# A second late token group kept turned in DRAM, and the raw second shared weights loaded behind the last expert tile

## The chip, the core and the metric

The kernel runs on one core of one Trainium2 chip. A core has TensorE (PE, matrix products, weight loads shown as PEld), VectorE (DVE), ScalarE (ACT) and GpSimd (POOL), and SyncE (SP), which here only issues transfers and counts their landings. Sixteen DMA engines carry the transfers. SBUF holds 128 partitions; matrix products land in eight PSUM banks of 128x512 values. The metric is device time in microseconds of one execution, as the median of several runs. A profiled execution gives the trace.

## What is computed

The input is 2 x 2048 tokens of 512 values (4096 tokens). Cut to what matters:

```python
# attention part (linear, no softmax over positions)
h = layernorm(X) * ln_w + ln_b;  Q, K, V = split(h @ W_in + b_in)
A = sum over positions of (K_rot / |K_rot|) * V
x = x + layernorm(X + (A * Q_rot) @ W_out + b_out)      # X = layernorm(x)
# FFN part, on xf = layernorm(x), 8 experts, the best 2 of each token
gates = softmax of the 2 largest of xf @ gate_w
routed = sum over the 2 experts of gate * (gelu(xf @ w1[e] + b1[e]) @ w2[e] + b2[e])
shared = gelu(xf @ shared_w1 + shared_b1) @ shared_w2 + shared_b2
out = x + layernorm(routed + shared)
```

`w1[e]` is 512x256, `w2[e]` 256x512, both shared weights are 512x512. Every large product is made with operands split in two parts, a high one and the rest (`_hi`, `_lo`), as three products: hi·hi, hi·lo and lo·hi.

## The kernel before

Tokens are worked on in eight groups of 512 (`G`), each of four tiles of 128. One program per engine is written out by hand, and each engine runs its own in order; semaphores (`wait_ge`, `then_inc`) tie them. Nothing reorders the work. A wait of SP holds back every transfer that SP issues behind it. The phases are:

1. **Front (to about 300 us).** Per group: normalization, transposes, K, V and Q. Expert and shared weights are split in units and stored in DRAM (`we_dram`, `ws_dram`).
2. **Middle (about 300 to 510 us), the loop `for s in range(NG)`.** Stage s makes the attention output of group s (`attend`), x2 and n3 (the FFN's input, `norm_x2`), and turns n3 of group s − 1 on PE (`n3_turn`, L1666) into `tp`; ACT copies it as `n_hi` (L761), DVE subtracts for `n_lo` (L1152). From these come the gate logits and, for the five groups in `EARLY` = (0, 2, 4, 6, 7), the shared part: h at one stage, output tiles at the next (`fill`). DVE copies each output tile into a buffer `fo` (L1186, `f_out`), and SP stores it to `f_dram` (`store_f`, L518). In the middle of the phase two `fo` buffers take turns, so the third copy of a stage waits for the first tile's store to have landed.
3. **Routing (about 510 to 565 us).** Tokens are sorted by expert into `NRT` = 72 row tiles, of which 71 are worked on.
4. **Expert phase (to about 821 us).** Per tile i: POOL gathers 128 rows, PE turns them and makes both products, ACT scales, POOL scatters with addition into `f_dram` (L1614). SP runs a loop over the tiles, waits for each scatter to land (L602), and slips in loads whose target has become free.
5. **Late phase (the last 85 us).** The shared part of the three groups in `LATE` = (1, 3, 5), called late groups 0, 1, 2, and the last normalization of all groups. `places` sets the order: h(0), h(1), o(0), h(2), o(1), o(2). h(i) has four products of 12 matmuls, written here h(i,m), each into a bank of PSUM: h(0,m) into banks 0, 1, 3, 4; for i above 0 h(i,m) into banks 3 and 4 in turn, so each waits for the gelu of the product two before it (`sc_free`). ACT makes the gelu (L887) and the high part (L891), DVE the low part (L1445). o(i) has four output tiles; each needs all of h(i) and the second shared weights in two parts (`c2_hi`, `c2_lo`). DVE adds the output tile to what lies in `f_dram` (loaded as `f[g]`, L591) and takes its statistics (L1476, L1478); ACT normalizes (L896), POOL or DVE add x2, and the result is stored.

Late group 0's turned parts, made at stage 2, are stored to `nt_dram` by SP (L527) and come back in the expert phase as `nc_hi[0]` and `nc_lo[0]`. Late groups 1 and 2 are loaded as plain n3 (`n3c`) and turned on PE in the late phase: `late_turn(1)` stands between h(0,1) and h(0,2), `late_turn(2)` between h(1,1) and h(1,2). The first shared weights come from DRAM in two parts (`c1_hi`, `c1_lo`). The second come raw, `c2_raw`, and are split by ACT (L901) and DVE (L1489) in four parts beside h(0). Space in SBUF is shared over time: the expert weights of expert e lie at 16e to 16e + 16 KB, and what the late phase loads goes there once an expert's tiles are done.

## Time and profile before

| | us |
|---|---|
| median of 3 runs | 904.56 (904.41 to 906.53) |
| profiled execution, its own time | 903.74 |
| its span | 901.9 |
| PE busy | 850.7 (94%) |
| DVE busy | 671.6 (74%) |
| ACT busy | 430.1 (48%) |
| POOL busy | 404.5 (45%) |
| HBM read and written | 118.23 MB, 93.11 MB |

The span runs from the first to the last instruction of the trace; the profiled execution's own time is 1.8 us longer than that. Busy time is the time in which an engine works on an instruction. The granted clock of PE (PEclk) is given as a share of full speed: 1.00 is 2.4 GHz, 0.50 is 1.2 GHz. In a timeline, what stands in brackets behind a row is how long the engine was idle before it and what ended that; a row without brackets followed its predecessor or waited for under 0.2 us. All times are us from the start of the span.

### The profile page before, as it was taken

The page shows a single profiled execution, that of the slowest core. Times are in us where ns is not written, and L with a number is a line of the kernel's source. Part 1 is how long each engine was busy: PE and PEld are TensorE (multiplying, and loading weights), DVE is VectorE, ACT ScalarE, POOL GpSimd, SP SyncE. Part 2 cuts the span into 40 slices and gives each one's busy share as a digit, 9 for nine tenths or more (in the row PEclk, how much of TensorE's full clock was granted, in tenths as well). Part 3 has the DMA queues.
Part 4 walks back from the last instruction along what each step waited for, and adds up shares of the span by engine and source line. Part 5 has one row for each costly group of instructions (what it writes and reads, how often), then busy time and mean ns, then how long its engine had stood idle before and what let it go on. Part 6 is the DMA issues. An engine that isn't in the chain of part 4 may idle for free.

```text
span 901.9 us, 14793 instructions
## 1 busy us (share of the span) xinstructions
PE 850.7 (94%) x4510; PEld 712.6 (79%) x4510; DVE 671.6 (74%) x1446; ACT 430.1 (48%) x815; POOL 404.5 (45%) x322
## 2 busy tenths in 40 slices
PE   4999999999999989999999885999999999999986
PEld 3888888878888778788888664888888888888865
DVE  6977989889879887687778596566666656665877
ACT  5235445336242243242413471566666666666564
POOL 1457567576565010000001001567677667762275
PEclk9999999999999999999999988999999999999998
DMA  9228878778749798758533988588888879888999
GB/s 322 98 104 314 296 263 328 268 284 315 252 158 401 309 382 308 288 209 324 187 129 102 398 324 264 107 220 166 142 142 170 197 155 166 148 136 203 370 250 220
DMA packets 88026, 212.30 MB, mean 235 GB/s; under 512 B 11576, under 2 KB 20024, under 8 KB 82576
## 3 DMA queue, kind: packets, MB, share of 16 engines
q1 hardware_dynamic: 63520, 166.61, 50.6%
q0 software_dynamic: 19360, 43.60, 26.3%
q10 hardware_dynamic: 5072, 1.15, 0.8%
q8 instruction: 41, 0.67, 0.3%
q14 instruction: 33, 0.27, 0.1%
HBM read 118.23 MB, written 93.11 MB: 234 GB/s over the span
## 4 chain that ended last, share of the span: by engine, by line
PE 55%; DVE 19%; issue 8%; DMA 6%; ACT 6%; POOL 5%; DVEq 0%; POOLq 0%; SPq 0%; ACTq 0%
PE bank L1671 6%; PE bank L1672 6%; PE bank L1673 6%; PE bank L1916 4%; PE bank L1901 4%; PE bank L1915 3%; PE bank L1914 3%; PE bank L1933 3%; PE bank L1931 3%; PE bank L1932 3%; DMA n_scratch<-picked 2%; DVE rot L976 2%; PE bank L1666 2%; PE bank L1923 2%; POOL rsn L1548 2%
## 5 line engine op out<-in xcount | busy, mean ns | idle before, releaser
L1614 POOL DMA_INDIRECT f_scratch<-ro,dst x71 | 112.5, 1585 | 54.5 <-SPq L602 24.7
L1606 POOL DMA_INDIRECT xr<-n_scratch,ids x71 | 70.2, 989 | 71.9 <-issue 44.1
L1408 DVE TENSOR_TENSOR ro<-bank,b2b 128x512 f32<-128x512 f32 x71 | 49.1, 692 | 67.6 <-PE bank L1933 55.7
L1671 PE MATMUL bank<-wkv_hi,h_hi 128*128 128x512 f32 x248 | 97.2, 392 | 0.0
L1673 PE MATMUL bank<-wkv_hi,h_lo 128*128 128x512 f32 x248 | 96.6, 389 | 0.0
L1672 PE MATMUL bank<-wkv_lo,h_hi 128*128 128x512 f32 x248 | 96.5, 389 | 0.0
L1914 PE MATMUL bank<-we,x_hi 128*128 x284 | 86.1, 303 | 0.5 <-DVE x_lo L1383 0.5
L667 ACT ACTIVATE sq<-kb 128x512 f32<-128x512 f32 x32 | 20.3, 634 | 130.1 <-DVE kb L979 130.1
L1916 PE MATMUL bank<-we,x_lo 128*128 x284 | 80.4, 283 | 0.0
L1915 PE MATMUL bank<-we,x_hi 128*128 x284 | 80.4, 283 | 0.0
L1541 POOL TENSOR_TENSOR acc<-acc,prod 128x512 f32<-128x512 f32 x32 | 57.6, 1798 | 8.7 <-DVE prod L992 8.7
L1383 DVE TENSOR_TENSOR x_lo<-bank,x_hi 128x512 fp32r<-128x512 f32 x71 | 49.1, 691 | 11.4 <-ACT x_hi L837 9.4
L1587 POOL TENSOR_TENSOR zr<-zv,half 128x4 f32<-128x4 f32 x8 | 8.1, 1010 | 109.0 <-DVE zv L1122 109.0
L1931 PE MATMUL bank<-we,g_hi 128*128 x142 | 56.3, 396 | 0.7 <-DVE g_lo L1395 0.7
L1534 POOL TENSOR_TENSOR rn<-ssq,half 128x1 f32<-128x1 f32 x32 | 27.7, 866 | 64.1 <-ACT sq L667 64.1
L1933 PE MATMUL bank<-we,g_lo 128*128 x142 | 56.4, 397 | 0.0
L1932 PE MATMUL bank<-we,g_hi 128*128 x142 | 56.0, 394 | 0.0
L1914 PEld LDWEIGHTS bank<-we,x_hi 128*128 128x128 f32 x284 | 54.0, 190 | 0.9 <-issue 0.9
L1673 PEld LDWEIGHTS bank<-wkv_hi,h_lo 128*128 128x128 f32 x248 | 46.5, 188 | 9.7
L1915 PEld LDWEIGHTS bank<-we,x_hi 128*128 128x128 f32 x284 | 54.2, 191 | 0.0
L1671 PEld LDWEIGHTS bank<-wkv_hi,h_hi 128*128 128x128 f32 x248 | 46.6, 188 | 9.6
L1672 PEld LDWEIGHTS bank<-wkv_lo,h_hi 128*128 128x128 f32 x248 | 46.6, 188 | 9.3
(248 smaller groups left out, 2490.7 us busy)
## 6 DMA issues: line engine op xcount, KB each, us to landing
xg<-in_X SPq DMA_DIRECT2D x15, 1024.0 KB, 7.9
we<-expert_scratch SPq DMA_DIRECT2D x6, 2048.0 KB, 13.6
w_lo<-in_w SPq DMA_DIRECT2D x16, 512.0 KB, 5.5
expert_scratch<-w_hi SPq DMA_DIRECT2D x16, 512.0 KB, 2.8
expert_scratch<-w_lo SPq DMA_DIRECT2D x16, 512.0 KB, 4.2
q_scratch<-qh SPq DMA_DIRECT2D x8, 1024.0 KB, 3.9
q_scratch<-qb SPq DMA_DIRECT2D x8, 1024.0 KB, 6.1
q_hi<-q_scratch SPq DMA_DIRECT2D x8, 1024.0 KB, 4.8
```

The source lines that it names most:

```text
L1541: pool.tensor_tensor(a, a, prod[j % 2][:, :], ALU.add).then_inc(acc_done, 1)
L1606: pool.indirect_dma_start(xr[u][:, :], None, n3_dram, bass.IndirectOffsetOnAxis(ids[:, i:i + 1], 0)).then_inc(row_in[u], 16)
L1614: pool.indirect_dma_start(f_dram, bass.IndirectOffsetOnAxis(dst[:, i:i + 1], 0), ro[i % NRO][:, :], None, compute_op=ALU.add).then_inc(r_s ...
L1671: pe.matmul(dst, hi(k), w_hi(k), start=(k == 0), stop=False)
L1672: pe.matmul(dst, hi(k), w_lo(k), start=False, stop=False)
L1673: last = pe.matmul(dst, lo(k), w_hi(k), start=False, stop=(k == KD - 1 and not more))
L1914: pe.matmul(out_h, x_hi[u][:, s], part_of(e, 0, k, H), start=(k == 0), stop=False)
L1915: pe.matmul(out_h, x_hi[u][:, s], part_of(e, 1, k, H), start=False, stop=False)
L1916: last = pe.matmul(out_h, x_lo[u][:, s], part_of(e, 0, k, H), start=False, stop=(k == KD - 1))
L1931: pe.matmul(oe_ps[u][:, :], g_hi[u][:, s], part_of(e, 2, k, D), start=(k == 0), stop=False)
L1932: pe.matmul(oe_ps[u][:, :], g_hi[u][:, s], part_of(e, 3, k, D), start=False, stop=False)
L1933: last = pe.matmul(oe_ps[u][:, :], g_lo[u][:, s], part_of(e, 2, k, D), start=False, stop=(k == KH - 1))
```

## The change

It does four things.

- **Stores.** Late group 1 (token group 3) is treated at stage 4 as late group 0 is at stage 2: its `n_hi` and `n_lo` are stored to `nt_dram`, which has a place for two groups. ACT waits for these stores before it writes `n_hi` of group 4.
- **Loads.** In place of the plain n3 of late group 1, four pieces of 512 KB of the turned parts are loaded at tiles 64 to 67 of SP's loop. `late_turn(1)`, its ACT copies and its DVE subtractions are gone. `nc_hi[1]` and `nc_lo[1]` move to 16 and 24 KB, `f[2]` and `f[3]` to 164 and 96 KB.
- **Raw second weights.** `c2_raw` moves from 16 to 80 KB. It is loaded behind SP's loop over the tiles and behind a wait for the last tile's product, where it was loaded at tile 66. It is split beside h(0,2), h(0,3), h(1,0) and h(1,1), where it was beside h(0,0) to h(0,3). The high part of late group 2 (`nc_hi[2]`, also at 80 KB) waits for the split.
- **Waits of SP.** The loads of `f` follow without waits for the split and for the transposes.

```diff
@@ placement
-        f = [at(f"f{g}", kb_, [P, GT, D]) for g, kb_ in enumerate((64, 104, 16, 24, 32, 40, 48, 56))]
-        n3c = [None, at("n3c1", 8 * LATE[1], [P, GT, D]), at("n3c2", 72, [P, GT, D])]
-        nc_hi, nc_lo = (... for n, kbs in (("nc_hi", (128, 164, 80)), ("nc_lo", (0, 96, 88))))
+        f = [at(f"f{g}", kb_, [P, GT, D]) for g, kb_ in enumerate((64, 104, 164, 96, 32, 40, 48, 56))]
+        n3c2 = at("n3c2", 72, [P, GT, D])
+        nc_hi, nc_lo = (... for n, kbs in (("nc_hi", (128, 16, 80)), ("nc_lo", (0, 24, 88))))
-        c2_raw = at("c2_raw", 8 * EARLY[1], [P, KS, D])
+        c2_raw = at("c2_raw", 80, [P, KS, D])
+        c2_in = {("h", 0, 2): (0,), ("h", 0, 3): (1,), ("h", 1, 0): (2,), ("h", 1, 1): (3,)}
@@ SP, stages of the middle
-                if s == LATE[0] + 1:
-                    sp.wait_ge(t2_free, 2 + t2_use(LATE[0], KD - 1) + 1)
+                if s - 1 in LATE[:2]:
+                    sp.wait_ge(t2_free, 2 + t2_use(s - 1, KD - 1) + 1)
                     for c, part in enumerate((n_hi, n_lo)):
-                        sp.dma_start(nt_dram[c], ...).then_inc(turned, 16)
+                        sp.dma_start(nt_dram[LATE.index(s - 1), c], ...).then_inc(turned, 16)
@@ SP, loop over the tiles and behind it
                 if i == NRT - E:
                     sp.wait_ge(oe_full, NRT - E)
-                    load_n3(1)
-                if i == NRT - E + 2:
-                    sp.dma_start(c2_raw[:, :, :], sw2.rearrange("(k p) d -> p k d", p=P)).then_inc(c_in[1], 16)
+                if i in range(NRT - E, NRT - E + 4):
+                    c, h = (i - NRT + E) // 2, (i - NRT + E) % 2 * 2
+                    sp.dma_start((nc_hi, nc_lo)[c][1][:, h:h + 2, :]..., nt_dram[1, c, :, h * G:(h + 2) * G]).then_inc(n3c_in[1], 16)
+            sp.wait_ge(oe_full, NRT - 1)
+            sp.dma_start(c2_raw[:, :, :], sw2.rearrange("(k p) d -> p k d", p=P)).then_inc(c_in[1], 16)
...
             load_f(EARLY[0])
             load_f(LATE[0])
-            sp.wait_ge(c_split, KS)
             for g in EARLY[1:]:
                 load_f(g)
-            sp.wait_ge(tc_full, KD)
             load_f(LATE[1])
             load_f(LATE[2])
-            sp.wait_ge(tc_full, KD * (len(LATE) - 1))
+            sp.wait_ge(tc_full, KD)
@@ ACT
-                    if g == LATE[0] + 1 and k == 0:
-                        act.wait_ge(turned, 32)
+                    if g - 1 in LATE[:2] and k == 0:
+                        act.wait_ge(turned, 32 * (LATE.index(g - 1) + 1))
...
             scale_row(PRE)
-            for k in range(KD):
-                nc_hi_part(1, k)
-            act.dma_start(n3c[2][:, :, :], n3_groups[LATE[2]]).then_inc(n3c_in[2], 16)
+            act.dma_start(n3c2[:, :, :], n3_groups[LATE[2]]).then_inc(n3c_in[2], 16)
             for what, i, m in places:
                 if what == "h":
                     gelu_c(i, m)
-                if (what, i) == ("h", 0):
-                    c2_hi_part(m)
+                for k in c2_in.get((what, i, m), ()):
+                    c2_hi_part(k)
@@ DVE
-            nc_lo_parts(1)
...
                 if what == "h":
                     hc_lo_part(i, m)
-                    if i == 0:
-                        c2_lo_part(m)
+                    for k in c2_in.get((what, i, m), ()):
+                        c2_lo_part(k)
@@ PE, late_h
                     pe.wait_ge(oe_free, 2 + NRT - 1)
-                    late_turn(1)
...
-                pe.wait_ge(tc_free, 4 + KD * i)
+                if i == 1:
+                    pe.wait_ge(n3c_in[1], 64)
+                else:
+                    pe.wait_ge(tc_free, KD)
```

How this stands in the programs is shown at three places. Line numbers of the changed kernel are about three higher for the same line.

SP at stage 4 of the middle phase, before. `fo0` is the buffer of output tile (2,0):

```order
L452 DMA q_hi0_162<-q_scratch 128x2048 [waits o_full]
L452 DMA q_lo0_160<-q_scratch 128x2048
L532 DMA we_233<-expert_scratch 128x2x1024 [waits zero_stored]
L518 DMA f_scratch<-fo0_178 128x512 [waits o_free]
L518 DMA f_scratch<-fo1_179 128x512 [waits o_free]
L538 DMA out_0<-z0_157 128x4x512 [waits x2_ready]
```

and in the changed kernel:

```order
L455 DMA q_hi0_162<-q_scratch 128x2048 [waits o_full]
L455 DMA q_lo0_160<-q_scratch 128x2048
L530 DMA turned_scratch<-n_hi_167 128x2048 [waits t2_free]
L530 DMA turned_scratch<-n_lo_168 128x2048
L535 DMA we_233<-expert_scratch 128x2x1024 [waits zero_stored]
L521 DMA f_scratch<-fo0_178 128x512 [waits o_free]
L521 DMA f_scratch<-fo1_179 128x512 [waits o_free]
L541 DMA out_0<-z0_157 128x4x512 [waits x2_ready]
```

The two stores of 1 MB stand ahead of the half expert load and of the output tiles' stores.

SP at the end of its loop over the tiles, before (`r_stored` counts landed scatters by buffer):

```order
L588 DMA n3c1_264<-n3_scratch 128x4x512 [waits r_stored3,r_stored0,r_stored1,r_stored2,oe_full]
L618 DMA c2_raw_284<-in_shared_w2 128x4x512 [waits r_stored1,r_stored2]
L591 DMA f0_256<-f_scratch 128x4x512 [waits r_stored3,r_stored0,r_stored1,r_stored2]
L591 DMA f1_257<-f_scratch 128x4x512
L591 DMA f2_258<-f_scratch 128x4x512 [waits c_split]
```

and in the changed kernel:

```order
L619 DMA nc_hi1_266<-turned_scratch 128x1024 [waits r_stored3,r_stored0,r_stored1,r_stored2,oe_full]
L619 DMA nc_hi1_266<-turned_scratch 128x1024 [waits r_stored1]
L619 DMA nc_lo1_269<-turned_scratch 128x1024 [waits r_stored2]
L619 DMA nc_lo1_269<-turned_scratch 128x1024 [waits r_stored3]
L622 DMA c2_raw_283<-in_shared_w2 128x4x512 [waits r_stored0,r_stored1,r_stored2,oe_full]
L591 DMA f0_256<-f_scratch 128x4x512
L591 DMA f1_257<-f_scratch 128x4x512
```

The loop's last waits for scatters, which stood at f0, stand at `c2_raw` now.

ACT at the start of the late phase, from the last scaled row, before. `hsc` is a gelu's result, `bank4` here is that of h(0,3):

```order
L856 ACTIVATE ro2_254<-ro2_254,gate_of_96 128x512 [waits gate_ready,oe_free,oe_full]
L864 ACTIVATE nc_hi1_267<-bank7 128x512 [waits tc_full]
L864 ACTIVATE nc_hi1_267<-bank2 128x512 [waits tc_full]
L864 ACTIVATE nc_hi1_267<-bank5 128x512 [waits tc_full]
L864 ACTIVATE nc_hi1_267<-bank6 128x512 [waits tc_full]
L907 DMA n3c2_265<-n3_scratch 128x4x512
L887 ACTIVATE hsc0_276<-bank0,sb1c_56 128x512 [waits sc_full]
L891 ACTIVATE hc_hi0_278<-hsc0_276 128x512 [waits sc_free]
L901 ACTIVATE c2_hi_274<-c2_raw_284 128x512 [waits c_in1]
L887 ACTIVATE hsc1_277<-bank1,sb1c_56 128x512 [waits sc_full]
```

and in the changed kernel, where the first rows are `L859` and the load of `n3c2`:

```order
L892 ACTIVATE hsc0_275<-bank0,sb1c_56 128x512 [waits sc_full]
L896 ACTIVATE hc_hi0_277<-hsc0_275 128x512 [waits sc_free]
L892 ACTIVATE hsc1_276<-bank1,sb1c_56 128x512 [waits sc_full]
L896 ACTIVATE hc_hi0_277<-hsc1_276 128x512 [waits sc_free]
L892 ACTIVATE hsc0_275<-bank3,sb1c_56 128x512 [waits hc_split,sc_full]
L896 ACTIVATE hc_hi0_277<-hsc0_275 128x512 [waits sc_free]
L906 ACTIVATE c2_hi_273<-c2_raw_283 128x512 [waits c_in1]
L892 ACTIVATE hsc1_276<-bank4,sb1c_56 128x512 [waits hc_split,sc_full]
L896 ACTIVATE hc_hi0_277<-hsc1_276 128x512 [waits sc_free]
```

The first copy of the second weights stands behind h(0,2) and ahead of the gelu of h(0,3).

## Rows read from the trace of the kernel before

**Rows 1.** Busy time by stretch: stretch, length, PE, PEld, DVE, ACT, POOL, PEclk, DMA, GB/s

```profile
430.00:500.00 70.00, 69.11 (x334) 56.93 (x332) 52.92 (x158) 23.95 (x37) 6.42 (x6) 1.00 0.44 156
```

**Rows 2.** Timeline of SP at stage 2: start, length, queue, line, transfer

```profile
349.45 0.33 SPq L452 DMA_DIRECT2D q_hi<-q_scratch  x1
...
350.30 0.43 SPq L527 DMA_DIRECT2D turned_scratch<-n_hi  x1
...
354.79 3.99 SPq L518 DMA_DIRECT2D f_scratch<-fo  x2
```

**Rows 3.** Timelines of DVE and PE at the end of stage 2

```profile
363.80 0.69 DVE L1186 COPY fo<-bank 128x512 f32<-128x512 f32 x1 [2.85 <-DMA f_scratch<-fo]
...
370.26 1.09 PE L1666 MATMUL bank<-ident,n 128*128 128x128 f32 x8 [1.48 <-ACT n L773]
```

**Rows 4.** Timeline of SP at stage 4

```profile
404.57 0.33 SPq L452 DMA_DIRECT2D q_hi<-q_scratch  x1
...
405.43 0.43 SPq L532 DMA_DIRECT2D we<-expert_scratch  x1
409.98 3.99 SPq L518 DMA_DIRECT2D f_scratch<-fo  x2
```

**Rows 5.** Timelines of DVE, ACT and PE at the end of stage 4

```profile
416.06 0.67 DVE L1186 COPY fo<-bank 128x512 f32<-128x512 f32 x1
...
419.52 2.94 ACT L773 ACTIVATE n<-z,xnm,xr__76 128x512 f32<-128x512 f32 x4 [12.52 <-DVE xnm L1145]
...
423.75 1.03 PE L1666 MATMUL bank<-ident,n 128*128 128x128 f32 x8
```

**Rows 6.** Busy time by stretch, at stage 4 (columns as in rows 1)

```profile
410.00:415.00 5.00, 5.00 (x22) 4.04 (x22) 4.02 (x8) 0.00 (x0) 0.00 (x0) 1.00 1.01 384
```

**Rows 7.** Timeline of SP at the end of the expert phase

```profile
812.07 0.37 SPq L588 DMA_DIRECT2D n3c<-n_scratch  x1
816.88 0.38 SPq L618 DMA_DIRECT2D c_raw<-in_shared_w  x1
833.23 12.87 SPq L591 DMA_DIRECT2D f<-f_scratch  x8
```

**Rows 8.** Chain of work that ended last, in order of time: start, length, what

```profile
825.04 8.10 DMA f_scratch<-ro,dst
...
833.23 5.60 DMA f<-f_scratch
```

**Rows 9.** Timeline of ACT beside h(0)

```profile
827.98 0.62 ACT L901 ACTIVATE c_hi<-c_raw 128x512 fp32r<-128x512 f32 x1
828.50 0.67 ACT L887 ACTIVATE hsc<-bank,sb1c 128x512 f32<-128x512 f32 x1
```

**Rows 10.** Timeline of PE: late_turn(1), h(0,2), h(1,1), o(0) and its second tile

```profile
824.13 1.91 PE L1666 MATMUL bank<-ident,n3c 128*128 128x128 f32 x16
825.79 0.48 PE L1974 MATMUL bank<-nc_hi,c_hi 128*128 128x512 f32 x1
...
834.05 0.39 PE L1974 MATMUL bank<-nc_hi,c_hi 128*128 128x512 f32 x1
...
843.98 0.39 PE L1671 MATMUL bank<-c_hi,hc_hi 128*128 128x512 f32 x1
...
846.70 0.39 PE L1671 MATMUL bank<-c_hi,hc_hi 128*128 128x512 f32 x1
```

**Rows 11.** Timeline of DVE: low part of h(1,3), first add of a late tile

```profile
846.05 0.67 DVE L1445 TENSOR_TENSOR hc_lo<-hsc,hc_hi 128x512 fp32r<-128x512 f32 x1
...
848.35 0.68 DVE L1476 TENSOR_TENSOR f<-bank,f 128x512 f32<-128x512 f32 x1
```

**Rows 12.** Busy time by stretch, around two falls of PE's clock (columns as in rows 1)

```profile
554.00:560.00 6.00, 0.00 (x0) 0.00 (x0) 1.04 (x5) 0.00 (x0) 2.41 (x3) 0.56 0.92 353
560.00:565.00 5.00, 4.23 (x18) 3.52 (x19) 2.53 (x4) 1.20 (x2) 0.00 (x0) 0.51 0.52 207
875.00:879.00 4.00, 3.73 (x9) 2.97 (x10) 3.35 (x12) 0.26 (x1) 3.58 (x5) 0.57 1.12 222
```

More of the change, by code:

```diff
@@ L244, in sandwich_kernel @@
         rank_ps, ids_ps = bank[2], bank[0]
-        tc = ((bank[7], bank[2], bank[5], bank[6]), (bank[1], bank[0], bank[7], bank[2]))
+        tc = (bank[1], bank[0], bank[7], bank[2])
         sc = (bank[0], bank[1], bank[3], bank[4])
@@ L523, in _ @@
                     load_q(s + 2)
-                if s == LATE[0] + 1:
-                    sp.wait_ge(t2_free, 2 + t2_use(LATE[0], KD - 1) + 1)
+                if s - 1 in LATE[:2]:
+                    sp.wait_ge(t2_free, 2 + t2_use(s - 1, KD - 1) + 1)
                     for c, part in enumerate((n_hi, n_lo)):
-                        sp.dma_start(nt_dram[c], part[:, :, :].rearrange("p k t -> p (k t)").bitcast(F32)).then_inc(turned, 16)
+                        sp.dma_start(nt_dram[LATE.index(s - 1), c], part[:, :, :].rearrange("p k t -> p (k t)").bitcast(F32)).then_inc(turned, 16)
                 if s in (3, 4):
@@ L595, in _ @@
             sp.wait_ge(f_stored[0], 16 * f_buf_uses[0])
[L596 to L597 removed]
+            sp.wait_ge(turned, 64)
+            sp.dma_start(nc_hi[0][:, :, :].rearrange("p k t -> p (k t)").bitcast(F32), nt_dram[0, 0]).then_inc(turned, 16)
             sp.dma_start(c1_hi[:, :, :].rearrange("p k h -> p (k h)").bitcast(F32), ws_dram[0, 0]).then_inc(turned, 16)
@@ L860, in scale_row_before, with nc_hi_part @@
                     scale_row(i - 2)
-            def nc_hi_part(i, k):
-                act.wait_ge(tc_full, KD * (i - 1) + k + 1)
-                act.activation(nc_hi[i][:, k, :], tc[i - 1][k][:, :], ACT.Copy).then_inc(nc_hi_done, 1)
+            def nc_hi_part(k):
+                act.wait_ge(tc_full, k + 1)
+                if k == 0:
+                    act.wait_ge(c_split, KS)
+                act.activation(nc_hi[2][:, k, :], tc[k][:, :], ACT.Copy).then_inc(nc_hi_done, 1)
             x_hi_part(0, 0)
@@ L1937, in expert @@
                 return pe.value_load(owner[0:1, i:i + 1], min_val=0, max_val=E - 1)
-            def late_turn_part(i, k):
-                pe.wait_ge(tc_free, KD * (i - 1) + k + 1)
-                transposes(tc[i - 1][k], n3c[i], k).then_inc(tc_full, 1)
             x_turn(0, 0, 0)
@@ L1958, in _, with late_turn @@
             h_turn(PRE, PRE % 2)
-            def late_turn(i):
-                pe.wait_ge(n3c_in[i], 16)
+            def late_turn():
+                pe.wait_ge(n3c_in[2], 16)
                 for k in range(KD):
-                    late_turn_part(i, k)
+                    transposes(tc[k], n3c2, k).then_inc(tc_full, 1)
             def late_h_part(i, m, lo):
@@ L1978, in _ @@
             pe.wait_ge(xt_free, PRE + 1)
-            pe.wait_ge(turned, 64)
+            pe.wait_ge(turned, 96)
             pe.wait_ge(c_in[0], 64)
```

31 lines of the change are left out of this document (14 added, 17 removed).

## The prediction, made before the changed kernel ran

> **What bounds the kernel now.** I read the busy shares by stretch first, then the timelines of SyncE (SP, which issues most transfers) and of the engines behind it, and last the chain of work that ended last. In the middle phase TensorE (PE) is the bound: it is busy 69.11 of the 70 us from 430 to 500 [rows 1], so an idle gap put into it there is not made up before the routing, and the routing and the 71 expert tiles follow it. The last 85 us are different. Their chain goes through the landing of the last scatter at 833.2 and the landing of f0 at 838.8 [rows 8], and then mostly through VectorE (DVE). PE works without a gap across that landing, since its late products need neither. So a shorter PE list at the end is worth little by itself; a new wait for something that lands near 838 is worth much.
>
> **Part 1, two more stores at stage 4.** SP now sends group 3's n_hi and n_lo (1 MB each) between the loads of q for stage 6 and the half expert load `we`. Issuing one costs SP 0.43 us [rows 2], about 1 for both, and no engine waits for that. What counts is what stands behind them: the 256 KB store of output tile (2,0). DVE's third copy of that stage writes the same buffer and waits for that store to land. Stage 2 already does the same thing, so its rows give the price. There q was issued at 349.45, the stores of the turned rows at 350.30 and after, the tile's store at 354.79 [rows 2], and DVE's copy waited 2.85 us and ran at 363.80 [rows 3]. That is 9.0 us after the issue of a 256 KB transfer, and 14.35 us after the q loads: the small store landed behind 4 MB.
>
> Stage 4 has the same line-up with `we` (1 MB) as well. From the q loads at 404.57 [rows 4]: 14.35, plus 1.05 MB at 384 GB/s [rows 6], 2.7 us, gives a landing at 421.6. From the other side: the copy at 416.06 ran without a wait [rows 5], so the store had landed by then; 2.10 MB more at 384 GB/s adds 5.5, at most 421.5. I take 421.5, so the copy is 5.4 us late. Behind it in DVE's list stand the last statistics, then GpSimd's root, ScalarE's (ACT) four normalizations and PE's transposes of them. At stage 2 the transposes began 370.26 − 363.80 = 6.46 us after the late copy, and PE had stood idle for 1.48 [rows 3]. At stage 4: 421.5 + 6.46 = 427.96, against 423.75 now with no gap [rows 5]. **PE stands idle 4.2 us**; between landings of 420.5 and 422.5 that is 3.2 to 5.2.
>
> A stall costs clock too. After a short gap the granted clock fell, near 875, from full (2.4 GHz) to half (1.2): the mean of 0.57 over four us is 3.4 us at half [rows 12], which loses 1.7. After the 6 us without a matmul from 554, the five that followed had 0.51, 4.9 us at half, a loss of 2.45 [rows 12]. For 4.2 us I take 1.7; I keep 0 to 2.45, as I can't tell from these rows what falls into a gap of this length. **Part 1: +5.9 us** (3.2 to 7.6). The wait that the change adds on ACT (group 4's n_hi must not be written before group 3's has left) comes after those same transposes, at 427.96 or later, when the stores, which stand ahead of the tile's store, have landed: 0, and what hides it is PE's gap.
>
> The trace and a price of the Trainium skill part here. DMA: Bandwidth & Descriptors, section "Anatomy of one DMA", gives a transfer of the GpSimd path about 2.0 us plus its bytes at 436 GB/s; read as the price of any transfer by itself, that is an estimate of 2.6 us for 256 KB, part 1 would be 0 and the sum 7.0 us. The section "Queues, rings and completion order" of that page of the Trainium skill says that each DMA engine takes a ring's entries in order and that the mark of completion lands after all earlier writes of that engine, and the 9.0 us of stage 2 agree with that.
>
> **Part 2, the second late group loaded ready-made.** Gone: 16 transposes on PE (824.13 to 825.79, 1.66 us [rows 10]), four ACT copies of 0.62 [rows 9] and four DVE subtractions, on engines that wait for PE there. In their place SP loads four pieces of 512 KB at tiles 64 to 67 instead of one 1 MB group and the 1 MB of raw weights. The first goes at 812.07 and the third at 816.88 [rows 7], the last between that and the end of the loop. It needs to be there when product h(1,0) begins. From h(1,1) at 834.05 to the first output tile at 843.98 stand three products and 1.66 of transposes [rows 10], so a product is 2.76 us; h(1,0) began at 831.3 and would now at 829.7. If it is late it is covered, since PE is held up anyway until 840 (below): 0. ACT issues the load of the third group's n3 directly behind the last scaled row, sooner than before, and the transposes that need it come later than before: 0.
>
> **Part 3, the raw second weights.** This decides. Before, `c2_raw` was issued at 816.88, in the loop [rows 7]. Now it stands behind the loop, and the loop's last pass waits for tile 70's scatter to land. That is where SP stands until 833.23, when it issues f0 [rows 7, 8]; the wait for the last tile's product that the diff writes there has then long been met. So the raw weights are issued at 833.23. A 1 MB load from there lands after 5.60 us, by f0's own: **838.8** [rows 8]. I keep 837.5 to 841, since the traffic ahead changes and eight f loads follow behind. By the same page and section of the Trainium skill, DMA: Bandwidth & Descriptors (2.0 us and 1.05 MB at 436 GB/s), it would be an estimate of 4.4 us, and the sum 1.2 less; I keep the row.
>
> ACT reaches the first `c2_hi` copy behind the gelu and the copy of h(0,2). PE has that product one product ahead of 829.7, at 827.0; gelu 0.67 and copy 0.62 [rows 9] make it 828.3, where ACT now stands until 838.8 (before, this copy ran at 827.98 with its data there). Queued behind it: the gelu of h(0,3). PE can do h(0,3) and h(1,0), but h(1,1) writes the bank that this gelu reads. So PE stops at 834.05 − 1.66 = 832.4 and goes on at 838.8 + 0.52 (copy) + 0.67 (gelu) + 0.1 = **840.1**; it began h(1,1) at 834.05 [rows 9, 10]. That is 6.05 late, with the 1.66 saved already in it. The stall of 7.7 us should drop the clock; between the two cases above, 2.1 us is lost after it, so PE begins the first output tile near 843.98 + 8.15 = 852.1. DVE hangs on that by ACT's gelu and copy of h(1,3), 1.3 together: 853.4, against 846.05 for that subtraction [rows 11], +7.4. DVE's first add of a late tile ran at 848.35, some 1.3 us after its product was done (PE had begun the next at 846.70) [rows 10, 11]. That lag shrinks, and takes up a little of the delay: +7.0 at that add, from where the tail is DVE's as before. The four subtractions of c2 (0.7 each, as the add of such a tile [rows 11]) fall into the time in which DVE waits for PE's late products, so they add nothing. f0 lands another 1.05 MB at 384 GB/s later, 2.7 us, at 841.5, and its first statistics stand behind three of the c2 copies and two gelus, near 843.5: no wait. **Part 3: +7.0 us**; without the clock's share and with a landing at 837.5 it is 3.6, with one at 841 and 2.45 of clock 9.5.
>
> **The sum:** 5.9 + 7.0 = 12.9 us. The profiled execution's own time is 903.74 (span 901.9), so 916.6 on that; the median of the runs is 904.56, so **917.4** for the median.
>
> **Rivals.**
> Only the end stalls (B): transfers of one queue overtake each other, so that the tile's store lands as it does alone. For it: the store at 409.98 had landed within 6.1 us behind 3 MB of loads [rows 4, 5]. Against: stage 2, where the stall of 2.85 is there [rows 3]. Time: 904.56 + 7.0 = 911.6.
> Only the middle stalls (C): the last scatter lands early enough, since less traffic runs beside it, and `c2_raw` is on the chip by about 831. It would have to end 7 us sooner than the 8.10 us it takes [rows 8]. Time: 904.56 + 5.9 = 910.5, perhaps less a little.
> Not slower (D): SP issues `c2_raw` once the last product is done, as the diff's own wait reads; that is before PE's transposes at 824.13 [rows 10], so it lands by 829.7; with the tile's store unhindered too, PE keeps its 1.66 us. It decides from a landing at 831.1 (832.4 less 1.3); every us later is one us of PE stall. Time: 904.56 − 1.66 = 902.9. Against: program order on SP, and the fact that f0, which follows the same last wait, was issued at 833.23 [rows 7].
> More than the forecast (E): the clock stays at half longer after both stalls, or the scatter shares its engines with the 512 KB pieces and lands later: 921 and above.
>
> **How the numbers follow.** Both stalls (A) 0.78, B 0.10, C 0.05, D 0.04, E 0.03. A runs from 6.8 us (3.2 + 3.6) to 17.1 (7.6 + 9.5), 911.4 to 921.7; its upper end needs every term at its worst. With B and C at 911.6 and 910.5 taken in, the range is 909.5 to 921.0, which leaves out D, E and a corner of A, under 2 in 10. A measurement of this kernel tells about 0.3% (2.7 us) from no change: A, B, C and E are slower, 0.94 with a little of each lost to the bound; D at 902.9 is within it, 0.04; 0.02 is left for faster.
>
> **What the profile of the changed kernel would show.** DVE's third `fo` copy of stage 4 waits 4 to 6 us for f_scratch<-fo; PE has a gap of about 4 us ahead of the next transposes, near 424, and half clock after it. The expert phase is as long as before, shifted by some 6 us. `c_raw` is issued in one row with f0, about 8 us behind the last scatter's issue. ACT's first c_hi waits some 10 us for a DMA, and PE has a gap of about 7.7 us ahead of an L1971 matmul with a release by ACT's gelu. I am wrong if the copy of stage 4 runs without a wait, if `c_raw` goes out well ahead of f0, or if the tail behind the first late add is shorter by more than 2 us than the 53.5 us from 848.35 to the end now.

## The result, and the profile after

The changed kernel takes 919.37 us (median of five runs, 914.83 to 920.9), the kernel before beside it 904.56 us (five runs, 904.09 to 906.53). The ratio is 1.0151, with an interval of 1.0128 to 1.0175: 13.7 us slower by the ratio. The forecast was 917.4, in a range of 909.5 to 921.0. The profiled execution of the changed kernel took 914.83, the lowest of the five, with a span of 912.9 (before: 901.9). Its rows show both stalls, and beside them an expert phase that was 3.3 us shorter than before.

Stage 4, SP, in the order of issue (start, us, engine and line, operation, out<-in, count). It answers to [rows 4]:

```profile
404.42 0.33 SPq L455 DMA_DIRECT2D q_hi<-q_scratch  x1
404.79 0.43 SPq L455 DMA_DIRECT2D q_lo<-q_scratch  x1
405.27 0.43 SPq L530 DMA_DIRECT2D turned_scratch<-n_hi  x1
405.74 0.65 SPq L530 DMA_DIRECT2D turned_scratch<-n_lo  x1
406.44 0.45 SPq L535 DMA_DIRECT2D we<-expert_scratch  x1
409.83 3.99 SPq L521 DMA_DIRECT2D f_scratch<-fo  x2
```

DVE and PE behind it, which answer to [rows 5]:

```profile
422.88 0.69 DVE L1189 COPY fo<-bank 128x512 f32<-128x512 f32 x1 [6.89 <-DMA f_scratch<-fo]
...
423.62 0.50 PE L1672 MATMUL bank<-wo_hi,q_hi 128*128 128x512 f32 x1 [2.59 <-DVE fo L1189]
...
429.33 1.09 PE L1667 MATMUL bank<-ident,n 128*128 128x128 f32 x8 [1.09 <-ACT n L776]
```

The store goes out at 409.83 and the copy that needs its buffer runs at 422.88, after a wait of 6.89 us; before it ran at 416.06 without one. PE has two gaps, 3.68 us in all. The first one I had not named: the next group's attention product wants the bank that the late copy empties. The transposes begin at 429.33, before at 423.75: 5.6 us.

The end of the expert phase and the late phase. SP, ACT and PE, answering to [rows 7], [rows 9] and [rows 10]:

```profile
815.30 1.60 SPq L619 DMA_DIRECT2D nc_hi<-turned_scratch  x2
819.79 4.69 SPq L619 DMA_DIRECT2D nc_lo<-turned_scratch  x2
836.07 0.38 SPq L622 DMA_DIRECT2D c_raw<-in_shared_w  x1
836.50 14.94 SPq L591 DMA_DIRECT2D f<-f_scratch  x8
...
841.18 0.63 ACT L906 ACTIVATE c_hi<-c_raw 128x512 fp32r<-128x512 f32 x1 [10.26 <-DMA c_raw<-in_shared_w]
...
842.44 0.79 PE L1971 MATMUL bank<-nc_hi,c_hi 128*128 128x512 f32 x1 [7.47 <-ACT hsc L892]
```

The raw weights are issued in one breath with f0. ACT stands 10.26 us for them, PE 7.47 us behind ACT's gelu. In the chain that ended last, the load of the raw weights (the second row below) now follows the last scatter (the first row), where f0 stood in [rows 8]; the others are the stretch behind the stall:

```profile
828.59 7.39 DMA f_scratch<-ro,dst
836.07 5.10 DMA c_raw<-in_shared_w
...
849.35 0.69 DVE hc_lo L1447
850.04 0.61 DVE c_lo L1491
850.74 0.61 ACT nc_hi L869
851.37 2.48 DVE nc_lo L1415 x4
```

Clock and traffic by stretch (from:to, length, busy us and count for PE, PEld, DVE, ACT and POOL, PEclk, DMA share, GB/s), answering to [rows 1] and [rows 12]:

```profile
424.00:428.00 4.00, 4.00 (x12) 2.86 (x10) 3.83 (x25) 1.66 (x3) 1.01 (x1) 0.58 0.82 319
430.00:500.00 70.00, 69.88 (x340) 58.01 (x339) 55.24 (x142) 22.13 (x35) 5.73 (x6) 1.00 0.41 148
842.00:848.00 6.00, 5.56 (x14) 4.29 (x15) 3.73 (x6) 3.30 (x7) 0.00 (x0) 0.51 1.02 388
875.00:879.00 4.00, 3.17 (x14) 2.27 (x14) 3.40 (x12) 2.87 (x5) 2.81 (x3) 1.00 1.10 181
```

The clock is at half behind both stalls: 0.58 over 424 to 428 is 3.4 us at half, which loses 1.7; after the late stall it is at half for some 5.2 us. From 430 to 500 PE is as dense as before.

### The profile page after: what moved, and what is told of

The parts are those of the page before. It is cut to its first block, busy times and chain, and to the rows that moved or that the text cites. A ratio compares the mean times of both kernels' runs of the same rounds, so it can differ in the third digit from the quotient of the medians.

```text
span 912.9 us, 14757 instructions
## 1 busy us (share of the span) xinstructions
PE 851.4 (93%) x4494; PEld 713.2 (78%) x4494; DVE 667.3 (73%) x1442; ACT 428.1 (47%) x811; POOL 404.7 (44%) x322
## 4 chain that ended last, share of the span: by engine, by line
PE 53%; DVE 19%; DMA 9%; issue 7%; ACT 6%; POOL 5%; POOLq 0%; DVEq 0%; ACTq 0%; SPq 0%
PE bank L1672 6%; PE bank L1673 6%; PE bank L1674 6%; PE bank L1932 3%; PE bank L1916 3%; PE bank L1917 3%; PE bank L1915 3%; PE bank L1934 3%; PE bank L1902 3%; PE bank L1933 3%; DMA f_scratch<-fo 2%; DMA n_scratch<-picked 2%; DVE rot L979 2%; DMA f_scratch<-ro,dst 2%; PE bank L1667 2%
## 5 line engine op out<-in xcount | busy, mean ns | idle before, releaser
L1411 DVE TENSOR_TENSOR ro<-bank,b2b 128x512 f32<-128x512 f32 x71 | 49.1, 692 | 73.5 <-PE bank L1934 68.5
L1672 PE MATMUL bank<-wo_hi,q_hi 128*128 128x512 f32 x128 | 52.2, 408 | 5.1 <-DVE fo L1189 2.6
L776 ACT ACTIVATE n<-z,xnm,xr__76 128x512 f32<-128x512 f32 x32 | 23.4, 804 | 67.2 <-DVE xnm L1148 67.2
## 6 DMA issues: line engine op xcount, KB each, us to landing
we<-expert_scratch SPq DMA_DIRECT2D x6, 2048.0 KB, 13.5
```

Source lines behind the costliest of these rows:

```text
L1672: pe.matmul(dst, hi(k), w_hi(k), start=(k == 0), stop=False)
```

## The experiments

Eleven kernels were timed beside the kernel before, and that kernel was profiled once more (c2). The kernel before had medians of 907.4, 906.2 and 907.1 in the three groups of runs, above the 904.56 of the first comparison, so each number is read against its own group: e1, e2, e3 and e6 against 907.4; c1, e5, e7 and e8 against 906.2; e9, e10, e11 and c2 against 907.1. A difference in us below is the ratio less one, times 906.

One table serves for all. It splits each profiled execution at two instants: the first transposes of the expert phase on PE, and L, SP's first issue behind its loop, which comes once the last scatter has landed. The last two columns are timed.

| kernel | expert phase begins | from there to L | L to the end | median | against before (interval) |
|---|---|---|---|---|---|
| before | 560.31 | 272.9 | 68.7 | 904.56 | |
| before once more (c2) | 563.23 | 271.5 | 71.4 | 907.1 | |
| changed | 566.42 | 269.7 | 76.8 | 919.37 | 1.0151 (1.0128 to 1.0175) |
| changed once more (c1) | 568.62 | 269.6 | 77.2 | 919.59 | 1.0149 (1.0122 to 1.0177) |
| e1 raw at tile 68 | 568.68 | 272.5 | 77.3 | 921.77 | 1.0160 (1.0123 to 1.0197) |
| e2 turned stores behind | 556.72 | 276.5 | 77.5 | 912.29 | 1.0048 (1.0029 to 1.0068) |
| e3 part 1 alone | 569.03 | 273.7 | 70.7 | 913.36 | 1.0066 (1.0045 to 1.0088) |
| e5 before, stores behind | 558.12 | 269.5 | 70.5 | 902.07 | 0.9955 (0.9937 to 0.9974) |
| e6 raw by ACT | 568.21 | 277.6 | 69.9 | 915.65 | 1.0079 (1.0050 to 1.0108) |
| e7 raw at tile 66 | 568.33 | 272.1 | 68.5 | 912.34 | 1.0065 (1.0044 to 1.0086) |
| e8 = e7 and stores behind | 558.48 | 271.7 | 68.5 | 901.10 | 0.9944 (0.9927 to 0.9962) |
| e9 part 2 alone | 560.12 | 277.8 | 68.6 | 909.24 | 1.0034 (1.0015 to 1.0052) |
| e10 turned stores by POOL | 566.47 | 277.2 | 75.8 | 920.43 | 1.0144 (1.0117 to 1.0171) |
| e11 raw behind f0 | 570.60 | 273.1 | 79.2 | 924.84 | 1.0201 (1.0174 to 1.0228) |

The kernels whose small store waits at stage 4 begin the expert phase at 566.4 to 570.6, the others at 556.7 to 563.2. From L to the end it is 75.8 us or more where the raw weights land late, and 71.4 or less in the others. The middle column varies by 8 us from one trace to the next; what the edits do to it is taken up with e9.

### The change again, and the kernel before again

> The changed kernel once more, unaltered, as the yardstick for the runs beside it. The kernel before ran at 907.4 beside the first four experiments, 2.8 us above the 904.6 of the first comparison. Theory (the 1.5% is a property of the change): 12 to 16 us above the kernel before, whatever that measures here. In its trace the stage 2 gap of PE decides a part: 1.68 us left the clock at full (transposes of the next stage 26.7 us later), 2.1 us and more in the three experiments dropped it (28.3 us).

> The kernel before, unaltered, for a second trace of it. Beside the experiments it measured 906 to 907, against 904.6 in the first comparison. Theory: PE's gap ahead of 370 is above 2 us here and drops the clock, so the next transposes begin 28.3 us later instead of 26.7, and the expert phase starts near 562.5 instead of 560.3. Rival: the difference lies in the expert phase alone.

c1 is 13.5 us above the kernel before (11.1 to 16.0): the result repeats. c2 is a single execution, 908.02 us; the 907.1 in its row of the table is the median of its group. The first of these rows is c2's, the second c1's:

```profile
371.17 1.51 PE L1666 MATMUL bank<-ident,n 128*128 128x128 f32 x8 [2.28 <-ACT n L773]
```

```profile
370.86 1.09 PE L1667 MATMUL bank<-ident,n 128*128 128x128 f32 x8 [2.26 <-ACT n L776]
```

And the stretch 368 to 376 of both, c2 first:

```profile
368.00:376.00 8.00, 5.72 (x23) 4.48 (x23) 7.17 (x14) 4.12 (x6) 0.00 (x0) 0.79 0.67 251
```

```profile
368.00:376.00 8.00, 5.74 (x34) 4.58 (x33) 7.90 (x13) 4.70 (x8) 0.00 (x0) 1.00 0.66 250
```

In c2 the gap of stage 2 is 2.28 us, the clock drops to half (0.79 as the mean of the stretch), and the next transposes come at 399.47, 28.3 us later. That is what the theory said. Against the first trace these transposes are 2.5 us later, and the start of the expert phase is 2.9 us later. So in this pair of traces stage 2 explains most of the difference at that point; that it explains the medians too, 2 to 3 us higher here, isn't shown by one more trace. In c1 a gap of 2.26 us left the clock at full (next transposes 26.7 us later). Over all traces with a gap of 2.1 to 2.5 there, the clock fell in c2, e1, e3, e6 and e11 and stayed in c1 and e7; with 1.48 to 1.76 (before, changed, e9) it stayed. So my expectation that everything over 2.1 us drops it was too simple.

### Part 1 alone (e3)

```diff
-                if s == LATE[0] + 1:
-                    sp.wait_ge(t2_free, 2 + t2_use(LATE[0], KD - 1) + 1)
+                if s - 1 in LATE[:2]:
+                    sp.wait_ge(t2_free, 2 + t2_use(s - 1, KD - 1) + 1)
                     for c, part in enumerate((n_hi, n_lo)):
-                        sp.dma_start(nt_dram[c], ...)
+                        sp.dma_start(nt_dram[LATE.index(s - 1), c], ...)
```

(on the kernel before; ACT's wait goes with it)

> The kernel before with part 1 alone: group 3's turned rows are stored at stage 4 as in the changed kernel and ACT waits for them, but nothing reads them; late group 1 is still turned on PE and the raw weights are loaded at tile 66. Theory: the middle is 5.6 us longer, as in the changed kernel; 904.6 becomes 910.2. Rival (the expert phase takes back about 3 us of a later start, as its rows in the changed kernel read): 907 to 908. Rival (parts overlap, the middle costs nothing at the end): 904.6.

Measured: 6.0 us slower (4.1 to 8.0). In its trace the third copy waits:

```profile
425.25 0.69 DVE L1186 COPY fo<-bank 128x512 f32<-128x512 f32 x1 [6.79 <-DMA f_scratch<-fo]
```

The late phase is untouched: 70.7 us from L, where the kernel before has 68.7 and 71.4. The loss arrives whole at the end, and the rival by which the expert phase takes half of it back falls. It had come from the changed kernel's first profile: its 269.7 us from the start of the expert phase to L (269.6 in c1) are at the low end of what the table shows, and e5, which has no stall, has 269.5.

### The stores behind the first two output tiles (e2, e5)

```diff
-                if s - 1 in LATE[:2]:
-                    ...                      # the stores of the turned rows
...
                 for g in late:
                     store_f(g, 0)
                     store_f(g, 1)
+                if s - 1 in LATE[:2]:
+                    ...                      # the same lines
```

> The changed kernel with the stores of the turned rows issued behind the stores of the stage's first two output tiles instead of ahead of them, at stages 2 and 4; all else as changed. Theory (the 256 KB store lands behind what was issued ahead of it on its queue): the third fo copy of stage 4 runs without a wait near 417, PE's two gaps before 430 and the half clock behind them go, about 5.6 us at stage 4, and the wait of 2.85 us at stage 2 goes too, with PE's 1.5 us there; 919.4 becomes about 912, or less. Rival (the delay comes from total traffic, whatever the order): the copy still waits about 4 us or more and the time stays near 919. Second rival: the middle gains 5 to 7 us but the expert phase gives half of it back, 915 to 916.

> The kernel before with one edit: at stage 2 the stores of group 1's turned rows are issued behind the stores of the first two output tiles. No part of the change is in it. Theory (a small store waits for what is ahead of it on its queue): the third fo copy near 361 does not wait, PE's gap ahead of 370 goes, and the expert phase starts 3.5 us earlier: 3 to 4 us below the kernel before. Rival (the expert phase, whose length varied by 6 us between executions, swallows it): no measurable difference.

e2 is 4.3 us above the kernel before where c1 is 13.5: 9.2 us of the changed kernel's time were the place of these stores on SP, at both stages. Not all of that is the change's cost, since the kernel before has the stores of stage 2 in the same place (e5 below). SP and DVE at stage 4 of e2:

```profile
408.19 3.99 SPq L521 DMA_DIRECT2D f_scratch<-fo  x2
412.23 0.43 SPq L539 DMA_DIRECT2D turned_scratch<-n_hi  x1
412.70 0.45 SPq L539 DMA_DIRECT2D turned_scratch<-n_lo  x1
...
414.27 0.67 DVE L1189 COPY fo<-bank 128x512 f32<-128x512 f32 x1
```

The copy runs without a wait, 6.1 us after the store's issue. e2's expert phase begins at 556.7, before even the kernel before (560.3), because stage 2's own stall is gone too. e5 shows that alone: the kernel before with stage 2's stores moved is 4.1 us faster (2.4 to 5.7). That leaves some 5 of the 9.2 us for stage 4, in line with e3's 6.0.

```profile
360.81 0.67 DVE L1186 COPY fo<-bank 128x512 f32<-128x512 f32 x1
...
368.57 1.04 PE L1666 MATMUL bank<-ident,n 128*128 128x128 f32 x8
```

Against [rows 3]: the copy at 360.81 instead of 363.80, the transposes at 368.57 without a gap instead of 370.26. The stage-2 row on which I priced part 1 was at the same time a place to save.

### Is it the queue? (e10)

```diff
-                (the stores of the turned rows on SP)
...
             for s in range(NG):
                 z_rsqrt(s)
+                if s - 1 in LATE[:2]:
+                    pool.wait_ge(t2_free, 2 + t2_use(s - 1, KD - 1) + 1)
+                    for c, part in enumerate((n_hi, n_lo)):
+                        pool.dma_start(nt_dram[LATE.index(s - 1), c], ...).then_inc(stored, 16)
                 x2_rsqrt(s)
```

> The changed kernel with the stores of the turned rows issued by POOL, on its own queue, behind its root of the stage's z (near 352 and 408), ahead in time of the output tile's store on SP's queue as before, but not ahead of it in that queue. Theory (what holds the small store back is the order within one queue): the third fo copy of stage 4 does not wait, or under 1 us; 919.6 becomes about 911. Rival (the sixteen engines serve whatever was issued first, whatever queue it is on, as much traffic stands ahead): the copy waits 4 us or more, and the time stays near 919.

The theory falls. POOL's issues, SP's issue of the small store, and DVE's copy:

```profile
406.38 0.60 POOL L1596 DMA_DIRECT2D turned_scratch<-n_hi  x1
406.97 0.53 POOL L1596 DMA_DIRECT2D turned_scratch<-n_lo  x1
...
408.63 3.99 SPq L521 DMA_DIRECT2D f_scratch<-fo  x2
...
421.41 0.69 DVE L1185 COPY fo<-bank 128x512 f32<-128x512 f32 x1 [6.62 <-DMA f_scratch<-fo]
```

The copy comes 12.8 us after the store's issue, in the changed kernel 13.05, and the time is the changed kernel's (1.0144 against 1.0149). The 2 MB on another queue hold the small store back as much as those on its own. The transfers issued from 400 on show why, with their median times to landing:

```profile
q_lo<-q_scratch SPq DMA_DIRECT2D x1, 1024.0 KB, 8.1
we<-expert_scratch SPq DMA_DIRECT2D x1, 1024.0 KB, 15.9
turned_scratch<-n_hi POOLq DMA_DIRECT2D x1, 1024.0 KB, 10.8
turned_scratch<-n_lo POOLq DMA_DIRECT2D x1, 1024.0 KB, 14.0
```

`we`, issued at 404.07 ahead of POOL's two, lands near 420, after 15.9 us, and POOL's land at 417 and 421. In the trace of the kernel before `we` landed 9.4 us after its issue. So transfers that left later on another queue held it back by 6.5 us: the queues share the DMA engines, and `we` and the small store behind it advance at a part of the rate. What counts is how many bytes are on their way beside the small store, on whichever queue. The Trainium skill says the same, DMA: Bandwidth & Descriptors, section "Issuing engines are not separate DMA queues": transfers of the scalar, sync and gpsimd engines end up on the same 16 DMA engines and interleave there. e10's row agrees, with 12.8 us.

At stage 2 the move did change something. POOL's two stores left at 352.45 and 353.22 there, some 2.5 us later than SP's, the copy waited 1.69 us (3.63 in c1), and PE's gap ahead of the transposes almost closed:

```profile
368.95 1.09 PE L1667 MATMUL bank<-ident,n 128*128 128x128 f32 x8 [0.31 <-ACT n L772]
```

That is why e10 begins the expert phase 2.1 us ahead of c1. The median, with an uncertainty of over 2 us, doesn't show it.

### The raw second weights (e1, e7, e6, e11)

e1 and e7 load them inside SP's loop, to another place in SBUF, and split them beside h(0,0) to h(0,3) as before; SP waits for the split again behind its third load of `f`. The two differ in the tile.

```diff
+                if i == NRT - E + 2:         # e7; e1 has NRT - E + 4
+                    sp.wait_ge(oe_full, NRT - E + 2)
+                    sp.dma_start(c2_raw[:, :, :], ...).then_inc(c_in[1], 16)
...
-            sp.wait_ge(oe_full, NRT - 1)
-            sp.dma_start(c2_raw[:, :, :], ...).then_inc(c_in[1], 16)
```

> Undoes part 3 alone: the raw second shared weights are loaded in SP's loop at tile 68, to the place of f[4], and split beside h(0,0) to h(0,3) as before the change; stores and loads of the turned rows stay as changed. Theory (the late stall is one mechanism, worth 7 us at the first late add): c_hi runs without a wait, no gap ahead of the L1971 matmul, and the median falls from 919.4 to about 912. Rival (the stall is covered, because the tail is DVE's and the last scatter's anyway): 917 or more. A third reading, that the ready-made group saves its 1.66 us at the end as well, would give about 910.5.

> Part 3 undone, in the way e1 should have been: the raw second shared weights are loaded at tile 66 of SP's loop, as in the kernel before, to the place of f[4], and split beside h(0,0) to h(0,3). In e1 SP reached tile 68 only at 836.9, since the last three scatters are issued and land together. Theory (the late stall is the raw weights' landing): c_hi without a wait, first late add 15 to 17 us after the last scatter's landing instead of 23.5, 8 us less than the changed kernel. Rival (part 2's pieces of 512 KB, not the raw weights, make the end late): 3 us less or nothing.

e1 won nothing (14.5 us above the kernel before), and its trace says why: tile 68 isn't early.

```profile
836.88 0.38 SPq L623 DMA_DIRECT2D c_raw<-in_shared_w  x1
841.13 15.66 SPq L591 DMA_DIRECT2D f<-f_scratch  x8
...
843.93 0.63 ACT L908 ACTIVATE c_hi<-c_raw 128x512 fp32r<-128x512 f32 x1 [11.64 <-DMA c_raw<-in_shared_w]
```

The scatters of tiles 68 to 70 can only go once an earlier tile's rows have landed (POOL waits 4.9 to 7.3 us there in every trace). They then go out within 4.2 us of one another, and in e1 SP gets past tile 68's landing and tile 70's 4.3 us apart, some 8 us after the issue of each. A load tied to tile 68 leaves 4.3 us ahead of f0; in the kernel before, at tile 66, it left 16 us ahead [rows 7]. At tile 66 (e7) it leaves at 824.26, 16 us ahead of f0, and c_hi runs at 833.36, before the scatter has landed. ACT still waits 4.9 us there, against the expectation, yet L to the end is 68.5, the lowest of the table: in the chain DVE's first statistics follow f0's landing, as before the change (the second row below). e7 is 5.9 us above the kernel before (4.0 to 7.8), c1 13.5: part 3 costs 7.6 us.

```profile
833.36 0.63 ACT L908 ACTIVATE c_hi<-c_raw 128x512 fp32r<-128x512 f32 x1 [4.89 <-DMA c_raw<-in_shared_w]
...
845.88 0.69 DVE L1470 BATCH_NORM_STATS2 fst<-f 128x6 f32<-128x512 f32 x1 [2.44 <-DMA f<-f_scratch]
```

e6 leaves the place and the split as changed and lets ACT issue the load behind the last scaled row:

```diff
+            act.dma_start(c2_raw[:, :, :], ...).then_inc(c_in[1], 16)
             act.dma_start(n3c2[:, :, :], n3_groups[LATE[2]]).then_inc(n3c_in[2], 16)
```

> The changed kernel with one transfer moved: ACT issues the load of the raw second weights, on its own queue, right behind the last scaled row and ahead of the load of the third late group's n3, instead of SP behind its loop. The split stays beside h(0,2) to h(1,1). Theory (SP's place behind the landing of the last scatter is the cause): issued near 824.5 it lands near 830, c_hi waits less than 1 us, PE's gap of 7.5 us goes; 919.4 becomes about 912. Rival (the transfer is slowed by the last scatters, whatever queue it is on): it lands near 835 and half of the gain is left, 915 to 916.

```profile
832.30 0.38 ACTq L907 DMA_DIRECT2D c_raw<-in_shared_w  x1
...
841.89 0.63 ACT L903 ACTIVATE c_hi<-c_raw 128x512 fp32r<-128x512 f32 x1 [2.85 <-DMA c_raw<-in_shared_w]
```

PE's gap is gone and L to the end is 69.9, so the late stall goes as the theory says; the load takes 9.6 us beside the last scatters, as the rival says of the transfer. By the ratios the time is 6.3 us below c1's, where e7 is 7.6 below; c_hi still waits 2.85 us, not under 1. The difference of 1.3 us is within the uncertainty of over 2 us that such a difference has, so theory and rival aren't told apart by the time, and one trace whose expert phase is among the longest doesn't do it either.

e11 exchanges two issues, f0 and the raw weights:

> The changed kernel with the raw second weights and f0 in the other order: SP issues f0 first behind the last scatter's landing, then the raw weights. Theory (what the late phase waits for is the raw weights): they land 2.7 to 5 us later than in the changed kernel, c_hi waits that much longer, and the time rises by 2.7 to 5 us to 922 to 925, although f0 is there sooner. Rival (the late phase waits for f0, the raw weights are beside it): the time falls by 2 to 3 us.

```profile
843.72 0.37 SPq L591 DMA_DIRECT2D f<-f_scratch  x1
844.14 0.50 SPq L626 DMA_DIRECT2D c_raw<-in_shared_w  x1
...
852.01 0.63 ACT L905 ACTIVATE c_hi<-c_raw 128x512 fp32r<-128x512 f32 x1 [13.01 <-DMA c_raw<-in_shared_w]
...
853.26 0.80 PE L1970 MATMUL bank<-nc_hi,c_hi 128*128 128x512 f32 x1 [10.22 <-ACT hsc L891]
```

c_hi waits 13.01 us and PE 10.22. In the first trace of the changed kernel it was 10.26 and 7.47, in c1's 11.34 and 8.55: 1.7 to 2.75 more in both. L to the end is 2.0 to 2.4 us longer, and the median 4.7 us above c1. f0's earlier landing gives nothing back. With the raw weights behind the last scatter, it is they that the late phase waits for, not f0.

### Part 2 alone, and both repairs together (e9, e8)

e9 is e7 without the stores of stage 4. Its pieces read late group 0's rows in `nt_dram`, so it leaves out late group 1's own rows and doesn't compute the result; it serves for its time alone.

> Part 2 alone: the kernel before with late group 1 loaded ready-made in four pieces at tiles 64 to 67 and its transposes, copies and subtractions gone, the raw weights at tile 66. Nothing more is stored at stage 4; the pieces read group 0's turned rows, so late group 1's shared part is computed from group 0's rows and is not the reference's. Theory (part 2 is worth 0, because the late phase hangs on the last scatter's landing and not on PE): within 1 us of the kernel before. Rival (the 1.66 us of PE transposes are saved at the end): 1.7 us below. Rival (the pieces delay the last scatters): 1 to 3 us above.

> e7 and e2 together: the raw weights at tile 66, and the stores of the turned rows behind the stores of the first two output tiles at stages 2 and 4. If the two stalls are separate their gains add: the changed kernel less 8 and less 9.5, which is 3 to 5 us below the kernel before, since stage 2's own wait goes too. Rival (they overlap, or the late phase hangs on the last scatter's landing, which the pieces delay by 1 to 3 us): level with the kernel before.

e9 is 3.1 us above the kernel before (1.4 to 4.7), so the theory of 0 misses and the rival by which the pieces delay the last scatters, 1 to 3 us above, fits. But the same part measured in other company costs nothing: e7 less e3 is −0.1, e8 less e5 −1.0, both with an uncertainty of over 2 us. At the median part 2 is worth between −1 and 3 us. That the 1.66 us of transposes are not saved is clear from e9 alone; the other two pairs leave room for it.

The traces show two things that take the saving back. In e7, e8 and e9 PE stands 2.13, 1.53 and 1.90 us ahead of h(1,0) for the last of the four pieces, which SP issues behind the raw weights; e9's row is

```profile
833.96 0.50 PE L1973 MATMUL bank<-nc_hi,c_hi 128*128 128x512 f32 x1 [1.90 <-DMA nc_lo<-turned_scratch]
```

And the last scatters are later. With 3 MB loaded at tiles 64 to 67 instead of 2, POOL's wait ahead of tile 68 and the time from the last scatter's issue to L are together 16.3, 15.9 and 16.4 us (e7, e8, e9). In the four traces with 2 MB and no pieces (before, c2, e3, e5) they are 13.2, 10.5, 11.8 and 11.9, in the other seven 13.1 to 15.4. Against that the way from L to the first late add is 15.0 us in all three, and with the transposes 15.1, 17.9, 17.2 and 17.0. In c2 and e5 the chain runs through PE's products and through both sets of transposes up to that add; this is c2's second set:

```profile
841.86 1.75 PE bank L1666 x16
```

So with part 2 the last landing came later in these traces, and what follows it sooner. How much is left at the end isn't settled by these runs: the phase ahead of it varies by more, 277.8 us up to L in e9 and 272.1 and 271.7 in e7 and e8 with the same pieces.

e8 is 5.1 us below the kernel before (3.4 to 6.6) and 18.5 us below the changed kernel beside it (c1), the fastest of the study. It is level with e5, the kernel before with four lines moved: the intervals overlap almost wholly. So the two stalls are separate and their repairs add up, and with both repaired the change still gains nothing that can be told from e5.

## Why the prediction was right, and where its steps were off

**The sum.** 12.9 us were forecast, 13.5 to 13.7 measured. Part 1 alone measures 6.0 (forecast 5.9), part 3 as c1 less e7 7.6 (forecast 7.0), part 2 between −1 and 3 (forecast 0); each has an uncertainty of about 2 us or more. Both stalls came where they were forecast and for the reason given. That the sum is right to within 1 us is in part luck, as the next paragraphs show.

**Part 1, the landing.** Forecast: the copy at 421.5, 5.4 us late. Measured 422.88, with a stage that ran 0.15 us earlier: 6.8 us late. Two terms were off and nearly cancelled. The landing was priced at 384 GB/s from the bytes issued up to the small store; it took another 1.4 us. From 404 to the copy 6.4 MB moved (339 GB/s over 18.88 us), and up to the small store 5.5 MB had been issued, so transfers issued behind it moved too. And 6.46 us were carried from stage 2 for the way from the copy to the transposes; here it is 429.33 − 422.88 = 6.45, but of the 4.2 us of idle PE only 3.7 are idle, since PE stood still earlier, for its bank, and then ran a product at half clock in the time I had counted as idle. The forecast of 4.2 idle and 1.7 of clock, 5.9, stands against 5.6 at 429.33, with the clock's 1.7 inside. The reason I gave for it, that the small store landed behind its own queue, was incomplete: e10 shows that bytes on another queue count the same. The sum had been made from bytes, so it survived this.

**Part 2, 0.** It held for the changed kernel, where PE is held up from h(1,1) on anyway. The more general premise, that the chain there goes mostly through DVE and PE's list is worth little, was read from one trace and isn't true of each: in c2, the same kernel, the chain goes through PE and both sets of transposes. And 0 was the right size without that stall too, for reasons I had not named: PE's wait of 1.5 to 2.1 us for the last piece, and later scatters (e9 above).

**Part 3, the issue.** SP issues the raw weights with f0, as forecast; landing after 5.10 us (5.60 forecast), c_hi's wait 10.26 (10.5), PE's gap 7.47 (7.7). h(1,1) begins 6.37 us after L, before 0.82 us after: 5.6 late, forecast 6.05. Then the mis-sized terms: the clock at half lasts from 842.4 to 847.6 and loses 2.6 instead of 2.1, and DVE's lag takes nothing back. I had put the four subtractions of c2 (the low parts, `c_lo`) at nothing. They are not: the chain has `c_lo` at 850.04 ahead of `nc_hi` (ACT must not write over the raw weights) and `nc_lo` behind it, and from 851.37 DVE works without a gap up to the first late add. From h(1,1) to that add are 17.2 us instead of 14.3. At the add the delay against L is 8.5, forecast 7.0. The 8.5 is one pair of traces; c1's add comes 22.7 us after L, against 15.1 to 17.9 in the four traces of kernels without parts 2 and 3.

**The tail as before.** From the first late add to the end 53.2 us (54.5 in c1), before 53.5. It held. The fall of the clock near 875 [rows 12] is absent after the change: the gap ahead of it, 1.83 us up to 875.27, is there again, 1.83 us up to 886.57, but the clock stays at full.

**The expert phase, as long as before.** In the profiled execution it was not: 3.3 us shorter up to L, which fits that this execution took 914.83 where the median is 919.37. Over fourteen traces this stretch takes 269.5 to 277.8 us whatever the edit. What makes it vary is open, but for the later last scatters of e7, e8 and e9. A single profile would have led me to believe that the expert phase returns half of the first stall; e3's median says it returns nothing.

**The rivals.** B (transfers of one queue overtake one another) and C (the scatter lands early) fall by the rows above. D (the raw weights go out by the last product) falls by the issue at 836.07. The estimate of 2.6 us for the small store was made from the price in the Trainium skill, DMA: Bandwidth & Descriptors, section "Anatomy of one DMA", read as that of any transfer by itself. It falls with B: the copy ran 13.05 us after the issue.

## What to carry to other kernels

A small store whose buffer is soon needed again should be issued ahead of every megabyte that can wait. Here that order alone decided 9 us of the changed kernel's time, of which 4 us were already lost in the kernel that was taken as tuned; changing the queue instead of the order gained nothing that the time shows. A load that sits behind a loop over landings is as late as the last landing, however early its own condition was met, and small moves in the list weigh much: the exchange with its neighbour f0 cost 4.7 us (e11), and two tiles sooner in the loop were worth 8.6 (e7 against e1): read where the issuing engine stands, not what the wait says. And where one stretch of a kernel varies by more than the effect, split each trace at fixed events, and leave the judgement of that stretch to medians.

## What the runs showed of the hardware

- A 256 KB store that leaves 4.6 us after the last of 3 MB of loads was done within 6.1 us; with 2 MB more issued ahead of it, 13.05 us passed until the copy that needed it (12.8 when those 2 MB were on POOL's queue). A 1 MB load issued ahead of POOL's 2 MB landed after 15.9 us instead of 9.4. It isn't the size of a transfer alone that sets its landing but what moves beside it.
- Gaps of the same length had different effects on TensorE's clock: 2.26 us left it at full, 2.28 us was followed by half; near the end, 1.83 us was followed by half in the trace of before and by full in that of after. At stage 2 the fall cost 1.6 us (28.3 against 26.7 to the next transposes), so a gap of about 2 us may or may not cost that much, in kernels whose programs are alike there.
- A scatter with addition that must wait for an earlier one's landing cost POOL 4.9 to 7.3 us of waiting ahead of tile 68 in every trace, and the last scatter, issued some 4 us later, took 5.6 to 10.4 us from its issue to SP's going on: 9.1 to 10.4 with 3 MB of loads beside the last tiles (e7, e8, e9), 5.6 to 8.2 with 2 MB (before, c2, e3, e5).
